# A four-GNN kernel: the order of the plain stage's work is drawn up anew

## The reference, cut to what matters

```python
edge_index = jnp.stack([src, dst])          # x: 50000 x 128, 25000 edges, dst sorted
h = jnp.maximum(_layernorm(x), 0.0)
x = x + _L0_gnn_ref(h, edge_index, ...)     # two GCN layers, 128 -> 256 -> 128
h = jnp.maximum(_layernorm(x), 0.0)
x = x + _L1_gnn_ref(h, edge_index, ...)     # two SAGE layers, relu
h = jnp.maximum(_layernorm(x), 0.0)
x = x + _L2_gnn_ref(h, edge_attr_16, ...)   # three layers with edge attributes
h = jnp.maximum(_layernorm(x), 0.0)
x = x + _L3_gnn_ref(h, edge_index, ...)     # four attention layers
return x
```

## Time and profile before

| | |
|---|---|
| median of 3 runs | 6344.36 us (6338.94 to 6345.71) |
| profiled execution, its own time | 6337.75 us |
| its span | 6336.0 us |
| TensorE busy, share of span | 4530.5 us, 72% |
| VectorE | 3780.2 us, 60% |
| ScalarE | 2726.0 us, 43% |
| GpSimd | 3542.5 us, 56% |
| granted TensorE clock, mean | 0.871 of full |

### The profile page before, as it was taken

The page is one execution under the profiler, slowest core; times in us unless marked ns, Lnnn a source line. Parts: engine busy times, 40 slices in busy tenths (PEclk is TensorE's granted clock), DMA queues, the critical chain, the costliest instruction groups (busy, mean ns, idle before and its releaser), DMA issues. The chain is left out here.

```text
span 6336.0 us, 129060 instructions
## 1 busy us (share of the span) xinstructions
PE 4530.5 (72%) x29783; PEld 3801.3 (60%) x29783; DVE 3780.2 (60%) x13813; ACT 2726.0 (43%) x6820; POOL 3542.5 (56%) x4340
## 2 busy tenths in 40 slices
PE   3777777777897679977999977665865876570165
PEld 2555555555786567776888866564754766570164
DVE  5666666666556863367666677535633643565576
ACT  2555555555233333355667666532332333230143
POOL 3445544444664737074757573175566567457576
PEclk9888888888897679988999988898998999895566
DMA  2444444444445755377333354493376359239543
GB/s 83 152 148 151 156 149 151 154 148 152 109 119 143 202 150 156 108 203 201 113 100 117 102 148 122 131 287 112 103 246 188 103 171 288 77 102 386 198 117 89
DMA packets 1087128, 971.55 MB, mean 153 GB/s; under 512 B 113208, under 2 KB 845962, under 8 KB 1087024
## 3 DMA queue, kind: packets, MB, share of 16 engines
q1 hardware_dynamic: 992944, 805.93, 40.3%
q0 software_dynamic: 94080, 164.48, 10.2%
HBM read 489.22 MB, written 484.70 MB: 154 GB/s over the span
## 5 line engine op out<-in xcount | busy, mean ns | idle before, releaser
L978 POOL DMA_INDIRECT G<-table,idx_all x1568 | 1555.8, 992 | 1073.3 <-issue 620.3
L1636 PE MATMUL PS<-G,S 128*128 (+2 forms) x4312 | 798.6, 300 | 4.4 <-DMA G<-table,idx_all 3.0
L978 POOL DMA_INDIRECT G<-table,idx_l x588 | 590.3, 1004 | 328.3 <-issue 177.9
L1636 PE MATMUL PS<-CR,LO 97*128 97x128 f32 (+1 forms) x4312 | 639.6, 296 | 86.1 <-ACT CR L1996 86.1
L1636 PEld LDWEIGHTS PS<-G,S 128*128 128x128 f32 x4312 | 686.2, 214 | 12.9 <-issue 3.8
L1636 PEld LDWEIGHTS PS<-CR,LO 97*128 97x128 f32 x4312 | 592.2, 210 | 151.9 <-ACT CR L1996 105.9
L1636 PE MATMUL PS<-G,FS 128*65 (+2 forms) x3234 | 515.9, 300 | 208.0 <-DVE den L1482 100.4
L1996 ACT ACTIVATE CR<-PS 65x128 f32<-65x128 f32 (+3 forms) x1078 | 289.1, 268 | 781.0 <-PE PS L1636 770.4
L928 POOL DMA_INDIRECT XIN<-in_x,idx_x x196 | 189.0, 964 | 690.8 <-ACT GN L1996 547.7
L1636 PEld LDWEIGHTS PS<-G,FS 128*65 128x65 f32 x3234 | 404.4, 151 | 274.8 <-issue 232.1
L1633 PE MATMUL PS<-ident,G 128*128 128x128 f32 x1372 | 249.7, 295 | 354.6 <-ACT G L1996 325.3
(11 more groups left out here) (315 smaller groups left out, 10270.5 us busy)
## 6 DMA issues: line engine op xcount, KB each, us to landing
table<-G SPq DMA_DIRECT2D x392, 256.0 KB, 2.8
table<-RO SPq DMA_DIRECT2D x343, 260.0 KB
table<-RO SPq DMA_DIRECT2D x245, 256.0 KB
OWN<-table SPq DMA_DIRECT2D x220, 260.0 KB
XIN<-xrows SPq DMA_DIRECT2D x196, 256.0 KB
table<-OWN SPq DMA_DIRECT2D x147, 260.0 KB, 3.4
OWN<-table SPq DMA_DIRECT2D x147, 256.0 KB
xrows<-RB SPq DMA_DIRECT2D x147, 256.0 KB
```

The source lines that it names most:

```text
L978: g.indirect_dma_start(G[:, t, 0:w], None, TAB[s], bass.IndirectOffsetOnAxis(ap=idx[:, t:t + 1], axis=0)).then_inc(gat[t % 4].sem, 16)
L1636: return nc.tensor.matmul(o, l, r, start=start, stop=stop)
```

## The change

Four of the five lists of the plain stage are reordered, and one computation is moved from one tile to another.

- The second norm, `norm(q1, 2)`, last but one on ScalarE, becomes `norm(q2, 2)`, second in the next iteration. The third root, `root(q2, 3)`, becomes `root(q3, 3)` in the next.
- `x_inverse` and `x_shift` move from q1 to q2, one iteration later.
- `constant` is added to the second sum's input (PX[2], once its norm has read it) and no longer to its output (PX[3]); so `xc` comes before `yx`, and who waited for `xc` now waits for `yx`.
- VectorE's, TensorE's and ScalarE's calls get a new order. SP keeps its order.

```diff
         q_v = {1: lagged("q_v1", ("stats", "aggr", "rs", "nb", "xb", "h1b", "x1")),
-               2: lagged("q_v2", ("stats", "aggr", "rs", "nb", "yx", "xc")),
+               2: lagged("q_v2", ("stats", "aggr", "rs", "nb", "xc", "yx")),
...
-                keep(q3, "x3", q_v[2], "xc", PX[3])
+                keep(q3, "x3", q_v[2], "yx", PX[3])
...
-                ready(dve, {1: (q_ld, q, "x"), 2: (q_v[1], q, "x1"), 3: (q_v[2], q, "xc")}[k])
+                ready(dve, {1: (q_ld, q, "x"), 2: (q_v[1], q, "x1"), 3: (q_v[2], q, "yx")}[k])
...
+            def constant(q):
+
+                if q is None:
+                    return
+                x_ = PX[2][q[2]]
+                ready(dve, (q_a[2], q, "g"))
+                done(q, 2, v.tensor_tensor(x_, x_, on4(c2_r[:, :]), ALU.add))
+
             def residual(q):
                 if q is None:
                     return
-                ready(dve, (q_p[2], q, "rB"), (q_st["x3"], earlier(q, 2), "x3"))
+                ready(dve, (q_p[2], q, "rB"), (q_v[2], q, "xc"), (q_st["x3"], earlier(q, 2), "x3"))
                 done(q, 2, v.scalar_tensor_tensor(PX[3][q[2]], bank(4), 0.0, PX[2][q[2]], ALU.max, ALU.add))
-
-            def constant(q):
-
-                if q is None:
-                    return
-                x_ = PX[3][q[2]]
-                ready(dve, (q_v[2], q, "yx"))
-                done(q, 2, v.tensor_tensor(x_, x_, on4(c2_r[:, :]), ALU.add))
...
             def plain(m, b):
                 q0, q1, q2, q3 = (earlier((m, 0, b), k) for k in range(4))
+                stats(q0, 1)
+                x_inverse(q2)
+                aggregate(q0, 1)
+                x_shift(q2)
+                with_bias(q1)
+                hidden(q1)
+                x_stats(q1)
                 inverse(q3, 3)
-                with_bias(q1)
+                inverse(q0, 1)
                 normed(q3)
-                stats(q0, 1)
-                aggregate(q0, 1)
-                x_stats(q1)
-                hidden(q1)
-                inverse(q0, 1)
-                x_aggr(q1)
                 shift(q0, 1)
                 convolved(q1)
-                attributes(q2)
-                residual(q2)
+                x_aggr(q1)
                 stats(q1, 2)
                 constant(q2)
                 aggregate(q1, 2)
-                x_inverse(q1)
+                residual(q2)
                 stats(q2, 3)
                 inverse(q1, 2)
-                x_shift(q1)
                 aggregate(q2, 3)
                 shift(q1, 2)
+                attributes(q2)
                 rows(q3, 8)
...
                 turned(q1, 1)
-                turned(q2, 2)
                 hidden(q1, 0)
                 hidden(q1, 1)
+                turned(q2, 2)
+                convolved(q1)
                 sampled(q2)
                 turned(q3, 3)
-                convolved(q1)
+                rows_b(q2)
                 attributes(q2)
-                rows_b(q2)
                 rows_a(q2)
                 rows(q3)
...
                 turned(q1, 1)
+                norm(q2, 2)
+                hidden(q1)
                 turned(q2, 2)
-                hidden(q1)
+                root(q3, 3)
+                root(q0, 1)
+                x_norm(q2)
                 sampled(q2)
                 turned(q3, 3)
-                x_norm(q2)
-                root(q0, 1)
                 norm(q0, 1)
                 convolved(q1)
+                root(q1, 2)
                 x_root(q1)
                 rows_a(q2)
-                root(q1, 2)
-                norm(q1, 2)
-                root(q2, 3)
```

## The result

The changed kernel takes 6512.4 us (median of 4 runs, 6495.5 to 6522.8) against 6345.0 for the kernel before: ratio 1.0263, 95% interval 1.0240 to 1.0286. It is 167 us slower; 6500 had been forecast. Three engines' lists have a new order (VectorE, TensorE, ScalarE), not four; in SP's only the step that the x3 store waits for has another name.

A forecast was written before the change was run, and what follows sets the result against it. The prediction took the plain stage to be bound by a loop through the late load, `hidden`, `convolved` and VectorE's tail. 38 us for order plus 118 for TensorE's clock gave 156, hence 6500 us, range 6440 to 6580.

The forecast's parts named there:

- The loop: Plain stage: copy, SP, load, statistics, `hidden`, TensorE's `convolved`, VectorE's tail, copy; 30.99 us a pair of iterations sets the pace.
- The norm's move: ScalarE's second norm, moved to the next iteration, runs beside the load and is not in the loop: zero gain.
- The third root: ScalarE computes the third stretch's root during the load's flight; VectorE needs it only after `hidden`: zero.
- `root(q0, 1)` ahead: ScalarE's root ahead of `x_norm`: the even iteration's wait goes, 3.52 becomes 2.38 before `convolved`, -1.14 us a pair.
- The head: VectorE, statistics to end of `hidden`: -0.18 us in the odd iteration, +0.56 in the even one.
- The tail: VectorE from `convolved` to copy's end, the residual waiting for `rows_b`: +0.76 us even, +0.78 odd.
- The order without the clock: Sum of root, head and tail terms in the plain stage: +0.78 us a pair, 38 us over 49 pairs.
- The gap before `convolved`: TensorE stands idle 4.5 us until `h1b`, longer than any wait the kernel before shows.
- The clock: TensorE's clock falls in the gap and slows `convolved` and following work: 1.2 us an iteration, 118 us over 98 iterations.
- The loads landed: Rival: the load lands sooner, 2.6 us after issue; with the clock kept 6295 us; chance 0.12.
- The clock was not kept: Rival "slower, clock kept": the gap falls so that `convolved` runs at the full level, 6382 us; chance 0.20.
- What the waits promised: Rival: TensorE sets the pace and 3.0 us an iteration go; at most 66 us, 6278; chance 0.04.

The follow-up runs named there:

- Run 1: The changed kernel with SP's load of the next quad issued one iteration earlier: 5944.1 us, ratio 0.9371 to the kernel before.
- run 8: The kernel before with ScalarE's `root(q0, 1)` put ahead of `x_norm`, one line of the change: 6348.7 us, ratio 0.9991.
- run 9: The kernel before with `root(q0, 1)` ahead, the second norm moved to the next iteration and first `hidden` ahead of second `turned`: 6292.8 us, ratio 0.9897.
- run 11: The kernel before with `root(q0, 1)`, second norm and first `hidden` moved, the load one iteration earlier and the third root in the next iteration: 6101.0 us, ratio 0.9591.
- run 4: The changed kernel with 18 unused matmuls on TensorE ahead of `convolved`: 6361.7 us, ratio 1.0006 to the kernel before.
- Run 7: The changed kernel with `sampled` ahead of `convolved` on TensorE and ahead of `root(q0, 1)` on ScalarE: 6476.0 us, ratio 1.0175.

## Why the prediction was right, and where its sizes were off

**The loop** was the one named. Its four pieces sum to the measured pair in both kernels. Run 1 takes 11.7 us off the pair: 8.5 of the load, 3.0 in front of `convolved` and 0.5 in the tail that are the clock's, less 0.3 in the head.

**The norm's move, put at zero.** With run 8 as its base it gave, with `hidden` moved ahead, 60 us (run 9), a part of it through a load that landed sooner. A loop through the norm, `turned` and `hidden` was only just shorter than the load's; the earlier trace rows would have shown it: in the even iteration `hidden` starts 1.39 us after the statistics, and VectorE alone needs 1.27. The lower level, read as lying beside the load, was on this loop too (`hidden` at 3.30 us instead of 1.98). So "the second norm is not in it" was true of the longest loop only, by a margin too small to build on. In the changed kernel this can't be told from the rest of the order.

**The third root, put at zero,** fits the late load by the loop; no run moved it alone there. With the load early it is worth 160 us in the old order on VectorE (run 11).

**`root(q0, 1)` ahead, -1.14 a pair.** In the new order, with the clock up, -1.31 (3.69 to 2.38 in the even iteration, run 4). By itself it gives nothing (run 8): the step needs more of the new order than its one line, and no run shows which part.

**The head, +0.56 and -0.18:** measured +0.52 and -0.18.

**The tail, +0.76 and +0.78:** with the clock up +0.59 and +0.62 (run 4). There the residual starts 2.81 after `convolved` where I had 2.90, and the steps behind it take 2.73 and 3.86 where I had 2.80 and 3.91. Handovers were counted a little too long. Run 7 shows that the wait is real.

**The order without the clock,** 38 us in the prediction: 4 us by run 4's ratio. This term was mis-sized by the tails, by the root, and by a load 0.16 us a pair shorter.

**The gap before `convolved`,** 4.5 us in the prediction: 4.94 in the row above, 5.03 on the mean. Its sum has a slip: the steps named there (0.6, 0.7, 2.0, 0.6, less 1.0) end 2.9 us after the copy and not 2.6. In the rows of the result TensorE starts 1.9 us before the copy's end (510.31 against 512.20) and ends 1.8 us after it; hence the longer gap.

**The clock, 1.2 us an iteration, 118 us in all:** by the pieces of the changed kernel and of run 4, 1.53 + 1.45 us in front of `convolved` and 0.17 + 0.42 in the tail, 3.57 a pair, 1.8 an iteration; by the ratios of the two runs 163 us, 1.7 an iteration. This is the term that was too small. What was measured is my upper bound of 1.7, half of a stretch of 3.4 us: the lower level fell onto the chain in every `convolved` that could be read (all 62 at 2.6 us or more), where I had let part of it fall into the gap. The Trainium skill (TensorE: Matmul & The Clock Gate, in its section on oscillation) describes just this pattern, short bursts of matmuls behind waits for transfers, each starting at the half rate. The trace agrees: 3.65 us for the 16 matmuls at 0.52 behind a gap of 4.94. The sum by that rule, 205 us, and mine, 156, lie on both sides of the 167.

The two errors, 34 us too much for the order and some 45 too little for the clock, cancelled for the most part. That the median came out 12 us from the forecast was luck to that extent; the mechanism was right, the two terms were not that good.

**The rivals.** The loads landed in 3.3 us (median, 300 to 700 us), the shortest in 2.7. The clock was not kept. What the waits promised is real only with the load early: the new order is then 5.6% faster than the old.

## What to carry to other kernels

Before an order is redrawn, find the transfer that a loop closes through: here it was issued behind the last store of an iteration, and both orders had to wait for it. The Trainium skill (DMA: Bandwidth & Descriptors, in its table of choices) says to issue early and wait late; moving that one call gave 8.7% in the changed kernel and 0.7% in the one before, and only with it did the new order pay. An engine's gap costs more than its length if TensorE's next work is on the loop, since that work then starts at the lower clock (3.56 us for a `convolved` instead of 2.02 here); look where the low stretch falls, not at its mean. An edit's worth is not a property of the edit: the same root gave nothing alone, the same `sampled` helped with the gap and hurt without it.

## What the runs showed of the hardware that I had not expected

- A shorter gap can go with a lower clock: with `with_bias` moved, the gap before `convolved` fell from 4.81 to 4.19 us, the granted clock of the stage in the profiled executions from 0.86 to 0.81, and 20 us of the expected 59 came; with 36 unused matmul instructions in the gap it stood at 1.00 and the gain came whole.
- These unused matmuls cost next to nothing where they fit: with 18 calls in each gap (4.18 us) `convolved` began 2.38 and 2.41 us behind `hidden`, where 2.38 is what TensorE alone sets, and the kernel was 2.5% faster than without. With 24 calls it began 2.60 and 3.14 behind it.
- The length of a gap alone did not settle the clock here: behind gaps of 2.5 to 3.1 us `hidden` was slow (over 2.3 us instead of 1.98) in 72 of 74 calls of the kernel before, and in run 9, behind gaps of 2.2 to 2.9, in 47 of 78; the 31 others had gaps of 2.3 to 2.9.
